# Order of the work around the first expert slot of a top-2 mixture-of-experts kernel: slot 0's high part in halves, and other places for a weight split, an index product and two DMA steps

## What is computed

```python
x = x + tanh(g_xattn[0]) * matmul(fake_quant(layernorm(x)), fake_quant(ctx))
n = layernorm(x)
logits = n @ W_gate + b_gate              # 8 experts
_, top_idx = top_k(logits, 2)
y_all = relu(einsum('bsd,edh->bseh', n, W_e) + b_e)
x = x + tanh(g_ffn[0]) * take_along_axis(y_all, top_idx[..., None], axis=2).mean(axis=2)
```

## Time and profile before

| | |
|---|---|
| median of three runs | 336.47 us |
| the profiled execution's own time | 337.47 us |
| its span, first to last instruction | 335.7 us |
| mean granted clock of TensorE | 0.963 |
| TensorE busy | 307.9 us (92%) |
| VectorE busy | 242.4 us (72%) |
| GpSimd busy | 184.1 us (55%) |
| ScalarE busy | 146.6 us (44%) |
| DMA | 81.49 MB, mean 243 GB/s |

### The profile page before, as it was taken

How to read it: one execution, slowest core, us unless ns; L and a number is a source line. 1 busy time by engine, 2 the same in 40 slices (tenths; PEclk the granted TensorE clock), 3 DMA queues, 4 the chain that set the end, 5 groups by cost and what they waited for, 6 DMA issues and landing times.

```text
span 335.7 us, 6287 instructions
## 1 busy us (share of the span) xinstructions
PE 307.9 (92%) x1601; PEld 233.3 (69%) x1602; DVE 242.4 (72%) x347; ACT 146.6 (44%) x147; POOL 184.1 (55%) x167
## 2 busy tenths in 40 slices
PE   4688999999979999999999999999999999999930
PEld 1233444786867888887888888888888888888820
DVE  2869999988798688599889576963559646963530
ACT  3769898945451911475447017410155006410110
POOL 5647535201002687687777557866548754876430
PEclk9999999979995999999999999999999999999985
DMA  6999945797674289899999978996449974365323
GB/s 215 414 409 386 401 184 170 272 379 256 242 267 174 80 275 327 203 278 349 402 355 338 385 209 193 328 343 174 79 132 340 298 198 110 93 137 113 60 81 62
DMA packets 19918, 81.49 MB, mean 243 GB/s; under 512 B 4160, under 2 KB 4160, under 8 KB 15808
## 3 DMA queue, kind: packets, MB, share of 16 engines
q1 hardware_dynamic: 12560, 58.76, 46.4%
q0 software_dynamic: 7200, 22.55, 29.1%
q10 hardware_dynamic: 144, 0.01, 0.0%
HBM read 62.43 MB, written 18.87 MB: 242 GB/s over the span
## 4 chain that ended last, share of the span: by engine, by line
PE 63%; DVE 15%; POOL 5%; DMA 5%; issue 4%; ACT 4%; DVEq 1%; ACTq 0%; SPq 0%; POOLq 0%
PE ps L1462 50%; POOL y_rows L510 4%; PE ps L1185 3%; PE ps_y L1214 3%; DVE w_lo L967 2%; DMA y_rows<-y_scratch,gidx 2%; DVE st L784 2%; PE ps_q L1242 2%; DMA stage<-in_ctx_dram 2%; PE ps_s L1238 2%; PE ps L1306 2%; DVE xt L840 2%; ACT u8c L569 1%; PE ps L1318 1%; POOL out_dram L532 1%
## 5 line engine op out<-in xcount | busy, mean ns | idle before, releaser
L510 POOL DMA_INDIRECT y_rows<-y_scratch,gidx x84 | 112.9, 1344 | 32.7 <-issue 25.0
L1462 PE MATMUL ps<-w_hi,yT_hi 128*128 x288 | 88.8, 389 | 0.8 <-DVE w_lo L967 0.8
L1462 PE MATMUL ps<-w_hi,yT_lo 128*128 x288 | 88.7, 389 | 0.0
L1462 PE MATMUL ps<-w_lo,yT_hi 128*128 x288 | 88.6, 389 | 0.0
L967 DVE TENSOR_TENSOR w_lo<-stage,w_hi 128x2048 f32 (+1 forms) x32 | 72.3, 2281 | 5.5 <-ACT w_hi L707 5.1
L698 ACT ACTIVATE yT_hi<-ps_y 128x1024 fp32r<-128x1024 f32 x21 | 21.6, 1027 | 123.7 <-PE ps L1462 69.3
L1462 PEld LDWEIGHTS ps<-w_hi,yT_hi 128*128 128x128 f32 x288 | 53.9, 188 | 12.5 <-issue 1.2
L1462 PEld LDWEIGHTS ps<-w_hi,yT_lo 128*128 128x128 f32 x288 | 54.1, 188 | 11.2
L1462 PEld LDWEIGHTS ps<-w_lo,yT_hi 128*128 128x128 f32 x288 | 54.1, 188 | 11.2
L532 POOL DMA_INDIRECT out_dram<-res,sidx x20 | 33.4, 1672 | 45.2 <-DVE res L1101 32.1
L707 ACT ACTIVATE w_hi<-stage 128x2048 f32 (+1 forms) x28 | 51.9, 1908 | 14.3 <-DMA stage<-in_L_ffn_W_e_dram 9.2
(11 more groups left out here) (200 smaller groups left out, 297.1 us busy)
## 6 DMA issues: line engine op xcount, KB each, us to landing
stage<-in_L_ffn_W_e_dram SPq DMA_DIRECT2D x32, 1024.0 KB
stage<-in_ctx_dram SPq DMA_DIRECT2D x16, 512.0 KB, 11.3
xt<-in_x_dram SPq DMA_DIRECT2D x8, 512.0 KB, 11.1
y_scratch<-y SPq DMA_DIRECT2D x8, 512.0 KB, 5.9
out_dram<-xt SPq DMA_DIRECT2D x8, 512.0 KB, 4.4
bias<-in_L_ffn_b_e_dram SPq DMA_DIRECT2D x8, 512.0 KB, 5.2
y_rows<-y_scratch,gidx POOLq DMA_INDIRECT x84
out_dram<-res,sidx POOLq DMA_INDIRECT x20
```

The source lines that it names most:

```text
L510: pool.indirect_dma_start(out=y_rows[q][:, b * QD:(b + 1) * QD], out_offset=None, in_=y_quarters[:, :], in_offset=bass.IndirectOffsetOnAxi ...
L1462: last = pe.matmul(ps[q][:, h * 512:(h + 1) * 512], lhs[q][:, k, :], w[:, bass.ds(woff + k * D + h * 512, 512)], start=(k == 0 and lhs is ...
```

## The change

On VectorE, the last quarter of expert 0's low split (`split_lo(3, ...)`) moves from behind `sign(1)` to ahead of `select(1)`; the copy of the last transposed logits moves from VectorE to ScalarE, behind `put_in_order(0)`. Slot 0's high part is copied in two halves, each with its own signal, and TensorE starts on the first half. `place_second` and `place_rows` take later places between slot 0's products. On GpSimd the scatter of slot 0 goes ahead of the gather of slot 3. On VectorE slot 2's turn goes ahead of split 1 of expert 1, and the bias and weigh of slot 1 go ahead of slot 3's turn. No instruction is added but the second half copy and the waits and signals that go with it.

```diff
--- before.py
+++ after.py
@@ -241,6 +241,8 @@
         s_lo = sem("w_lo_done")
         s_gi = sem("slot_indices_ready")
         s_pp = sem("params_step")
+        s_tph = sem("first_rows_turned_by_halves")
+        s_ehh = sem("first_rows_hi_half_ready")
         s_perm = sem("first_rows_in_order")
         s_g = [sem(f"gathered{q}") for q in range(2)]
         s_tp = sem("slot_yT_in_psum")
@@ -533,10 +535,10 @@
                                         out_offset=bass.IndirectOffsetOnAxis(ap=sidx[:, q:q + 1], axis=0),
                                         in_=res[q][:, :], in_offset=None, compute_op=ALU.add).then_inc(s_sc, 16)
 
+            pool.wait_ge(s_post, 1)
+            scatter(0)
             pool.wait_ge(s_gi, 2)
             gather(1)
-            pool.wait_ge(s_post, 1)
-            scatter(0)
             pool.wait_ge(s_gi, 3)
             gather(0)
             pool.wait_ge(s_sc, 16)
@@ -717,7 +719,11 @@
 
             act.wait_ge(s_first, 16)
             put_in_order(0, res[0])
-            evacuate_hi(0, yE_hi)
+            keep_logits(NT - 1, NT)
+            act.wait_ge(s_tph, 1)
+            act.activation(yE_hi[:, 0:KT // 2, :], ps_y[:, 0:KT // 2, :], ACT.Copy).then_inc(s_ehh, 1)
+            act.wait_ge(s_tp, 1)
+            act.activation(yE_hi[:, KT // 2:, :], ps_y[:, KT // 2:, :], ACT.Copy).then_inc(s_eh, 1)
             for i in range(TPB, NT):
                 add_rowsum(i)
             act.wait_ge(s_g[1], 16)
@@ -857,9 +863,6 @@
                 if g == 0:
                     dve.wait_ge(s_gate, e)
                 else:
-                    dve.wait_ge(s_gate, e)
-                    dve.wait_ge(s_gc, 1)
-                    dve.tensor_copy(logits_T[:, NT - 1 - TPB, :], ps_g[0:E, (NT - 1 - TPB) * P:(NT - TPB) * P]).then_inc(s_gc, 1)
                     dve.wait_ge(s_lgt, g)
                 dve.tensor_tensor(u(lg), gates_in[g][:, 0:n * E].rearrange("p (i e) -> p i e", e=E),
                                   bg.unsqueeze(1).to_broadcast([P, n, E]), ALU.add).then_inc(s_lg, 1)
@@ -1030,9 +1033,9 @@
                 make_onehot(i)
             split_lo(2, 3, slice(2 * CW, 3 * CW))
             read_rowsums(1)
+            split_lo(3, 4, slice(3 * CW, 4 * CW))
             select(1)
             sign(1)
-            split_lo(3, 4, slice(3 * CW, 4 * CW))
             positions(1)
             first_onehot(1)
             slot_matrix(1)
@@ -1110,17 +1113,17 @@
             dve.wait_ge(s_free, 3)
             weigh(0, fl(W0))
             split_lo1(0)
+            turn_rows(0, 1)
             split_lo1(1)
-            turn_rows(0, 1)
             evacuate_lo(2, yT_lo[0])
             split_lo1(2)
-            dve.wait_ge(s_el, 3)
-            turn_rows(1, 1)
-            split_lo1(3)
             dve.wait_ge(s_mm, 2)
             add_bias(1, 0)
             dve.wait_ge(s_free, 4)
             weigh(1, fl(W1))
+            dve.wait_ge(s_el, 3)
+            turn_rows(1, 1)
+            split_lo1(3)
             evacuate_lo(3, yT_lo[1])
 
             def step(slot, q, turn):
@@ -1297,6 +1300,8 @@
                     if k % (KT // HB) == 0:
                         pe.wait_ge(s_perm, slot * HB + 1 + k // (KT // HB))
                     last = pe.transpose(ps_y[:, k, :], in_order[slot][:, k * P:(k + 1) * P], ident_f[:, :])
+                    if slot == 0 and k == KT // 2 - 1:
+                        last.then_inc(s_tph, 1)
                 last.then_inc(s_tp, 1)
 
             def products(q, lhs, w, first, end):
@@ -1413,22 +1418,22 @@
             turn_logits(TPB, NT, 2)
             pe.wait_ge(s_ye, NT)
             turn_first(0)
-            place_rows(0, 1, 2)
             pe.wait_ge(s_xn, NT)
             pe.wait_ge(s_hi, NCH)
+            pe.wait_ge(s_ehh, 1)
+            products(0, yE_hi, w_hi, 0, KT // 2)
+            counts(1)
             pe.wait_ge(s_eh, 1)
-            products(0, yE_hi, w_hi, 0, 2)
-            counts(1)
-            products(0, yE_hi, w_hi, 2, KT)
+            products(0, yE_hi, w_hi, KT // 2, KT)
+            pe.wait_ge(s_lo, 4)
+            products(0, yE_hi, w_lo, 0, 2)
             place_second()
-            place_rows(0, 2, TPB)
-            pe.wait_ge(s_lo, 3)
-            products(0, yE_hi, w_lo, 0, 2)
+            products(0, yE_hi, w_lo, 2, 3)
+            place_rows(0, 1, TPB)
+            products(0, yE_hi, w_lo, 3, 4)
             place_rows(1, 4, 6)
-            products(0, yE_hi, w_lo, 2, 4)
+            products(0, yE_hi, w_lo, 4, 6)
             place_rows(1, 6, NT)
-            products(0, yE_hi, w_lo, 4, 6)
-            pe.wait_ge(s_lo, 4)
             products(0, yE_hi, w_lo, 6, 7)
             pe.wait_ge(s_abs, 1)
             for b in range(NQ):
```

## The result

The changed kernel takes 338.47 us (median of 13 runs, 337.3 to 339.89) against 336.47 in the runs of before beside it: a ratio of 1.0048, with a 95% interval of 1.0028 to 1.0069. It is slower, by 1.6 us on that ratio; a gain of 0.8 us was forecast. The profiled execution took 338.79, with a span of 337.0; before it was 337.47 and 335.7, so the pair of traces differs by 1.3 us.

A forecast was written before the change was run, and what follows sets the result against it. TensorE's unbroken work from 155.83 us fixes the end, so only reaching it earlier counts, via TensorE's work and the gather-to-split chain. Gain 131.8 - 131.0 = 0.8 us, from 336.47 to 335.7; range 334.0 to 337.4.

The forecast's parts named there:

- Up to slot 0's end: TensorE, VectorE and ScalarE ahead of slot 1: earlier first product and R, slot 0 ending at 112.2, gain 1.85 us.
- GpSimd's issues: Slot 0's scatter from about 115.3, then slot 3's gathers, lengthened by VectorE's splits; last gather issued by 126.7, 5.1 us later.
- The landing: Slot 3's gathered rows reaching SBUF 4.3 us after the last issue, at 131.0; bounds 3.2 and 5.9 us.
- L: Time when slot 3's gathered rows land in SBUF, forecast 131.0; VectorE turns them 0.1 us later.
- What follows from L: Slot 3's start: low part done at L + 4.7, new TensorE wait of 1.8 us, total gain 131.8 - L.
- The other strand: VectorE's path to expert 2's last split: slot 4's turn at L + 5.0, last quarter usable at L + 23.8.
- The sum: Whole kernel: 131.8 - 131.0 gives a gain of 0.8 us, from the median of 336.47 to 335.7.
- The one on the other side: Slot 3's first product: GpSimd's reorder costs more than TensorE wins; L 132.6, end 0.8 us later, 337.3; chance 0.20.
- The lower clock: Slot 0's end: lower level until 113 instead of 109.6 adds 1.7 us, giving 337.4; within the slower chance of 0.20.
- Slots 5 and on shift with it: TensorE behind slot 4: no waits there, feeding work moves along, so the 0.8 us gain stays.
- The rule of the Trainium skill: VectorE tensor_tensor with two SBUF inputs contends only with GpSimd's reads; inferred descriptor generation not held, so GpSimd's order costs nothing.

The follow-up runs named there:

- the repeat: The changed kernel run again unaltered, beside other runs on one chip; ratio 1.0043 to the kernel before.
- the fastest version: Changed kernel with GpSimd's order of before, slot 2's turn back behind expert 1's split 1, and split 3 behind slot 3's low part; ratio 0.9918 to before.
- the run with the clock kept up: Changed kernel with 16 idle matmuls on TensorE ahead of slot 3's wait; ratio 1.0030 to the kernel before, 1.0009 when run once more.

## Why the prediction was wrong

The direction was wrong and the time fell outside the range (338.47 against 334.0 to 337.4). TensorE was to reach its unbroken stretch, slot 4's last quarter, near 155.0; it reached it at 157.14. The steps, in their order:

**Up to slot 0's end: right in its places, lucky in its gain.** First product 92.20 (said 92.25), positions 94.62 (94.6), R on time, second index product 97.20 (97.2), token numbers 103.70 (103.8), quarter indices 106.40 (106.5), slot 2's gathers 107.94 (107.8). The gain was 3.4 us and not 1.85, because the clock did not fall near 103 in this execution. It did in the repeat, and at equal clock the gain was 1.2.

**GpSimd's issues: right in themselves, 0.9 us short in their start.** The scatter and two gathers met splits 0, 1 and 2 as worked out, each at its place, and from the scatter's start to the last issue's end passed 11.35 us (said 11.4). But the scatter was to begin 3.1 us behind slot 0's end, "an estimate that matters little"; it began 4.0 behind it (114.62 against 110.64; 3.9 in the repeat), behind slot 1's low part, the bias and the weigh.

**The landing: right by luck.** Taking L as the turn's start less 0.1, L was 131.2 (said 131.0). Three errors cancelled: slot 0 ended 1.6 us earlier than said, the scatter began 0.9 later behind that, and the rows came 5.2 behind the last issue and not 4.3 (bounds 3.2 to 5.9). Counted from slot 0's end, L came at 20.5 us and not at 18.8. In the repeat, where the clock did fall, L was 132.8.

**What follows from L: wrong, and this is the step that failed.** The prediction said "the low part is done at L + 4.7", "TensorE ... waits until L + 4.8" and "the gain is 131.8 - L", and took slot 3 to run at full speed. The low part was done at L + 4.7 (135.84); TensorE started 0.53 behind it, and not 0.1. The wait became 3.69 us (said 1.8): 0.9 from the scatter, 0.9 from the landing, 0.4 from this start, less small terms. Behind it the clock was at its lower level for 3.4 us, which puts 1.7 us on slot 3. I had put a lower clock only on slot 0's end, and had given a wait of 1.8 us no price. With 19.04 us of work and 1.7 of clock behind 136.37, TensorE comes to slot 4's last quarter at 157.1 instead of 155.83: the whole 1.3 us of the two spans. Of the 2.1 us between the forecast 155.0 and this, 1.7 are the clock and 0.4 the start.

**The other strand was mis-sized too.** "A step of 0.3 behind that VectorE turns slot 4's rows at L + 5.0": the turn began at 137.43, 1.6 us behind the low part with no releaser but "issue" in the row. The trace shows register and branch instructions there from 135.4 to 137.3: VectorE's first entry into the slot loop, with its loads of the number of slots and of the slot's entry. Before, this lay under the wait for the rows (132.1 to 134.5), and in the fastest version it lies under split 3. So without the fall of the clock the time would have been 0.4 us over before (137.43 + 18.8 = 156.2), not under it; the run with the clock kept up agrees, with its 0.25 us wait at that place (136.32 + 18.8 = 155.1).

**The sum.** From its own terms the gain was 132.0 - L (155.83 less L + 23.8); it was rounded to 131.8 - L, 0.2 us on the careful side, which changes nothing above.

**The rivals.** The one on the other side was right in its place, the wait at slot 3's first product, and in half of its price: it said 337.3 at L = 132.6. It came at L = 131.2 and cost more. I gave it 0.20. The lower clock was named as well, at another place. "Slots 5 and on shift with it" was wrong in general: the run with GpSimd's old order was 3.4 us ahead at slot 4 and lost 2.5 of them at slots 7 and 8.

**The rule of the Trainium skill** (SBUF — State Buffer, Who interferes with whom) on VectorE's two SBUF inputs was set aside in the prediction for the rows; the run with splits from PSUM now measures the same directly, 2.40 and 2.97 against 1.00 and 0.95. What it was set aside for is its inference on descriptor generation; an indirect DMA's read of its indices may fall under its rule on GpSimd's reads.

## What to carry to other kernels

Price a wait on the bounding engine twice: its length, and what its clock does behind it; a wait of 3.7 us here was followed by 1.7 us of lost clock, and one of 2.4 us by a fall as well. When a queue's instruction is moved ahead of others, work out for each one behind it which other engine's instruction it will now meet, and look at the first hand-over and the last: the order that was best here lets GpSimd's issues fall into VectorE's gaps and the next weight load come behind the last gather's issue, and it came from moving the split and not the DMA. Count a chain from the event that starts it (here slot 0's result), not from a fixed time: what is won ahead of that event neither covers the chain nor is eaten by it. A hidden stretch, such as the first entry into a loop, is a price to be set down before its cover is taken away.

## What the runs showed of the hardware

TensorE's clock fell to the lower level behind each wait of 3.25 to 3.7 us ahead of slot 3 (four traces of four), stayed there for 3.4 us, and did not fall when 16 constant matmuls filled the wait. It also fell behind a wait of 2.4 us in slot 4, in the one trace that has such a wait. Waits of 0.25 to 1.6 us in the slots had no such fall behind them.

A VectorE tensor_tensor of 2.28 us with both operands in SBUF holds an indirect DMA's issue on GpSimd (0.95 us) that starts inside it until 0.8 us behind its end: 2.40 and 2.97. With the second operand in PSUM the same length of work leaves it at 0.95 to 1.00. The landing of slot 3's gathers goes from 1.9 us behind the last issue's end to 4.9 when SyncE's weight loads of 1024 KB are in flight. Slot 0's scatter lands 7.1 to 10.8 us behind its issue's start (six traces).
